# Layer norm's chain, the first gate block, the token shift and one mask placed elsewhere in a fused attention and feed-forward kernel

## The reference

```python
x = x + ffn(cond(x, cond_2048, ...))          # x: (128, 32, 128) float32
# cond: convolution, layer norm, a 32-step recurrence, gate, output product
# ffn, six layers, each:
def attn_layer(x, Wqkv, qs, ksc, Wo):         # 16 heads of 64, windows of 32 tokens
    q, k, v = split(x @ Wqkv)                 # 128 -> 3 * 1024
    q, k = l2norm(q) * qs, l2norm(k) * ksc    # then rotary, scaled by position
    out = softmax(mask(q @ k.T * 8)) @ v
    return out @ Wo
def ffn_layer(x, g, bln, W1, b1, W2, b2):
    xn = layer_norm(x) * g + bln
    a, gate = split(xn @ W1 + b1)             # 128 -> 2 * 341
    return a * gelu(gate) @ W2 + b2
for i in range(6):
    x = attn_layer(shift_tokens(x), ...) + x  # shift: half of the channels come from the token before
    x = ffn_layer(shift_tokens(x), ...) + x
```

## Time and profile before

| | us |
|---|---|
| three runs, median (lowest to highest) | 2849.02 (2846.26 to 2850.98) |
| the profiled execution | 2847.98 |
| its span | 2846.2 |
| in it, TensorE busy | 2691.9 (95%) |
| VectorE busy | 2600.1 (91%) |
| ScalarE busy | 2246.7 (79%) |
| GpSimd busy | 2116.7 (74%) |

### The profile page before, as it was taken

The page is one execution under the profiler, slowest core; times in us unless marked ns, Lnnn a source line. Parts: engine busy times, 40 slices in busy tenths (PEclk is TensorE's granted clock), DMA queues, the critical chain, the costliest instruction groups (busy, mean ns, idle before and its releaser), DMA issues.

```text
span 2846.2 us, 92826 instructions
## 1 busy us (share of the span) xinstructions
PE 2691.9 (95%) x36416; PEld 2060.1 (72%) x36417; DVE 2600.1 (91%) x3375; ACT 2246.7 (79%) x3776; POOL 2116.7 (74%) x1529
## 2 busy tenths in 40 slices
PE   8799978999999999999999999999999999999996
PEld 7577756777777777777777777777777777777774
DVE  7899968999999999999999999999999999999993
ACT  5799957878788787878888787888878787887873
POOL 6766658777778777778777787777787777877771
PEclk9899999999999999999999999999999999999998
DMA  1000013232223332223232232222322322322222
GB/s 57 24 2 2 1 35 76 67 76 69 67 69 75 73 73 66 69 71 75 66 79 69 66 75 71 72 67 70 76 67 68 79 62 68 72 67 58 64 66 79
DMA packets 103719, 178.41 MB, mean 63 GB/s; under 512 B 29350, under 2 KB 52708, under 8 KB 103396
## 3 DMA queue, kind: packets, MB, share of 16 engines
q1 hardware_dynamic: 102372, 174.60, 25.2%
q10 hardware_dynamic: 1152, 1.20, 0.1%
HBM read 22.62 MB, written 2.10 MB: 9 GB/s over the span
## 4 chain that ended last, share of the span: by engine, by line
PE 30%; POOL 16%; issue 15%; ACT 11%; DMA 7%; DVE 5%; SPq 1%; POOLq 0%; ACTq 0%; DVEq 0%
PE pa L843 9%; POOL spare L1446 8%; DMA kT<-spare 7%; PE px L872 5%; PE pg L982 3%; PE ps L903 3%; PE pg L960 3%; PE px L917 3%; PE pg L974 2%; POOL xs_lo L1432 2%; DVE ss L1269 2%; ACT spare L1095 2%; POOL pr L1484 2%; ACT spare L1041 1%; POOL spare L1455 1%
## 5 line engine op out<-in xcount | busy, mean ns | idle before, releaser
L1446 POOL TENSOR_TENSOR spare<-spare,qk_t 128x1024 f32<-128x1024 f32 x384 | 910.1, 2392 | 10.9 <-POOL xs_lo L1432 8.1
L843 PE MATMUL pa<-w_hi,xs_hi 128*128 128x512 f32 x1152 | 511.9, 444 | 25.3 <-issue 8.6
L1462 POOL TENSOR_TENSOR sm<-sm,inv 128x512 f32<-128x512 f32 x192 | 201.8, 1051 | 429.2 <-DVE sm L1307 361.4
L1285 DVE TENSOR_TENSOR qk_t<-pa,rot 128x1024 f32<-128x1024 f32 x384 | 464.6, 1210 | 1.6 <-ACT spare L1048 0.8
L1276 DVE TENSOR_TENSOR spare<-pa,rot 128x1024 f32<-128x1024 f32 x384 | 464.6, 1210 | 0.0
L1269 DVE TENSOR_REDUCE ss<-spare 128x16 f32<-128x1024 f32 x384 | 457.7, 1192 | 6.1 <-ACT spare L1041 5.2
L843 PE MATMUL pa<-w_hi,xs_lo 128*128 128x512 f32 x1152 | 459.2, 399 | 0.3 <-DMA pT<-prT 0.3
L843 PE MATMUL pa<-w_lo,xs_hi 128*128 128x512 f32 x1152 | 455.0, 395 | 0.0
L872 PE MATMUL px<-ident_sb,spare 128*128 128x128 f32 x3072 | 407.2, 276 | 18.8 <-POOL spare L1455 11.9
L1455 POOL TENSOR_TENSOR spare<-spare,inv 128x1024 f32<-128x1024 f32 x192 | 365.9, 1905 | 69.6 <-ACT inv L1080 65.3
L872 PEld LDWEIGHTS px<-ident_sb,spare 128*128 128x128 f32 x3072 | 340.4, 140 | 105.1 <-issue 44.6
(11 more groups left out here) (178 smaller groups left out, 5926.1 us busy)
## 6 DMA issues: line engine op xcount, KB each, us to landing
kT<-spare SPq DMA_DIRECT2D x384, 256.0 KB, 3.7
pT<-prT SPq DMA_DIRECT2D x768, 64.0 KB, 2.0
w_part<-in_Wqkv SPq DMA_DIRECT2D x40, 192.0 KB, 3.7
wo<-in_Wo SPq DMA_DIRECT2D x6, 512.0 KB, 5.5
c_h<-in_x SPq DMA_DIRECT2D x4, 512.0 KB, 9.5
spare<-in_x SPq DMA_DIRECT2D x8, 256.0 KB, 4.8
out<-spare SPq DMA_DIRECT2D x8, 256.0 KB, 2.5
wo<-in_W SPq DMA_DIRECT2D x6, 341.0 KB, 5.2
```

What stands on the lines that cost most here:

```text
L843: last = pe.matmul(pa[(u + c) % 2][:, half * 512:half * 512 + 512], x[:, j * P:(j + 1) * P], w[:, at], start=(k == 0), stop=(k == 2))
L1285: dve.tensor_tensor(halves(qk_t[:, c, :]), halves(pa[(3 * j + c) % 2][:])[:, :, ::-1, :], table.unsqueeze(1).to_broadcast([P, HEADS, 2, DH ...
L1446: pool.tensor_tensor(qk_r[:, c, :], qk_r[:, c, :], qk_t[:, c, :], ALU.add)\
```

## The change

Five things, all in `stack`:

1. The chain of layer norm. TensorE's `variance` goes from behind the key transposes of step 0 to between the two halves of `project_k` of that step. ScalarE's `log_variance` goes ahead of `square_k`, and `round_normed` ahead of `floor_norms` and `copy_v`. VectorE's `normalise` goes ahead of the key's `sum_squares`, and `rest_of_normed` ahead of `rest_of_outputs`.
2. `gate_block(i, 2, 0)` goes from behind `scores` and `transpose_q` of step 1 to ahead of `scores`, right behind `project_q`.
3. The shift is done in three parts (256, 128 and 128 tokens). ScalarE does the second at step 3 of the body before and the third at step 0, behind `inverse_deviation`; GpSimd likewise, behind `norm_keys`.
4. The mask of the scores of step 1 is written by a bf16 matmul of TensorE in front of them, and ScalarE no longer writes it at step 0.
5. The reciprocal of the denominators goes behind `rest_of_outputs` at steps 0, 1 and 2.

```diff
-        HALF_TOK = 2 * P
+        SHIFT_PART = ((0, 2 * P), (2 * P, P), (3 * P, P))
...
-                def project(i, j, c, full, l, before_last=None):
+                def project(i, j, c, full, l, before_last=None, between=None):
...
                     for half in range(2):
+                        if between and half == 1:
+                            between()
...
-                        if j % 2 == 0:
-                            pe.wait_ge(s["xs_ready"], 4 * i + j + 2)
+                        if j != 1:
+                            pe.wait_ge(s["xs_ready"], 6 * i + (2 if j == 0 else 2 * j))
...
-                        project(i, j, 1, "k_full", l)
+                        project(i, j, 1, "k_full", l, None, (lambda: variance(i, 2)) if j == 0 else None)
+                    elif j == 0:
+                        variance(i, 2)
...
-                def scores(i, j, back):
-                    n, j, live = tile(i, j, back)
-                    if live:
-                        if isinstance(n, int) and n == 0:
+                def scores(i, j_now, back):
+                    n, j, live = tile(i, j_now, back)
+                    if live:
+                        if j_now == 1:
+                            pe.wait_ge(s["sub_done"], n)
+                        if j_now == 1 or isinstance(n, int) and n == 0:
                             pe.matmul(ps[:], ident_b[:], mask_b[:], start=True, stop=False, skip_group_check=True)
-                        wait_for(pe, s["masked"], n)
+                        else:
+                            pe.wait_ge(s["masked"], {0: i * 3 - 1, 2: i * 3, 3: i * 3 + 1}[j_now])
...
                         project_q(i, j, l)
+                        if j == 1:
+                            gate_block(i, 2, 0)
                         if j == 2:
                             a_block(i, 2, 1)
                         scores(i, j, 2)
                         if j == 0:
                             subtract_mean(i, 2)
                         transpose_q(i, j, 1)
-                        if j == 1:
-                            gate_block(i, 2, 0)
...
                         transpose_k(i, j, 1)
-                        if j == 0:
-                            variance(i, 2)
...
# ScalarE
                         if j == 0:
-                            shift_hi(i, 0, 1)
-                        if j == 2:
-                            shift_hi(i, -1, 0)
+                            log_variance(i, 2)
+                        if j >= 2:
+                            shift_hi(i, -1, j - 2)
...
-                        if j == 0:
-                            log_variance(i, 2)
...
-                        write_mask(i, j, 1)
+                        if j > 0:
+                            write_mask(i, j, 1)
                         if j == 0:
                             inverse_deviation(i, 2)
+                            shift_hi(i, 0, 2)
                         exponentials(i, j, 2)
...
                         copy_oT(i, j, 3)
+                        if j == 0:
+                            round_normed(i, 2)
                         floor_norms(i, j, 0)
...
-                        if j == 0:
-                            round_normed(i, 2)
# VectorE
                         times_cos(i, j, l, 1, "sq_k", "tk_done", "cos_k")
+                        if j == 0:
+                            normalise(i, 2)
                         sum_squares(i, j, 0, 1, "sq_k", "sum_k")
                         if j == 3:
                             add_attention(i, 1)
-                        if j == 0:
-                            normalise(i, 2)
                         if j == 1:
                             gated(i, 2, 0)
                         denominators(i, j, 2)
+                        if j == 0:
+                            rest_of_normed(i, 2)
+                        if j == 3:
+                            reciprocals(i, j, 2)
                         rest_of_outputs(i, j, 3)
+                        if j < 3:
+                            reciprocals(i, j, 2)
                         if j == 1:
                             gated(i, 2, 1)
-                        if j == 0:
-                            rest_of_normed(i, 2)
# GpSimd
                         if j == 0:
-                            shift_lo(i, 0, 1)
+                            shift_lo(i, 0, 2)
+                        if j == 3:
+                            shift_lo(i, -1, 1)
```

More of the change, by code:

```diff
@@ L1133, in tables, with shift_hi @@
                         act.preload_act_table_set(name)
-                def shift_hi(i, back, half, first=False):
+                def shift_hi(i, back, part, first=False):
                     g, live = group(i, back)
@@ L1138, in shift_hi @@
                     if live:
-                        at = bass.ds((g % GROUPS) * GTOK + half * HALF_TOK, HALF_TOK)
-                        to = slice(half * HALF_TOK, (half + 1) * HALF_TOK)
+                        first_tok, toks = SHIFT_PART[part]
+                        at = bass.ds((g % GROUPS) * GTOK + first_tok, toks)
+                        to = slice(first_tok, first_tok + toks)
                         act.wait_ge(s["res_ready"], g + 1)
-                        wait_for(act, s["v_full"], g * GT - 2 * (1 - half))
+                        wait_for(act, s["v_full"], g * GT - (2 - part))
                         act.copy(xs_hi[0:64, to], res[0:64, at]).then_inc(s["xs_hi_ready"], 1)
@@ L1259, in _ @@
                         shift_hi(0, 0, 1, True)
+                        shift_hi(0, 0, 2, True)
                 group_steps(act, body, lambda l: None)
@@ L1314, in denominators, with reciprocals @@
                         dve.reduce_sum(den[:], keys(pr[:]), AX.X).then_inc(s["den_done"], 1)
+                def reciprocals(i, j, back):
+                    n, j, live = tile(i, j, back)
+                    if live:
                         dve.wait_ge(s["den_done"], n + 1)
@@ L1424, in _, with shift_lo @@
             def _(pool):
-                def shift_lo(i, back, half, first=False):
+                def shift_lo(i, back, part, first=False):
                     g, live = group(i, back)
@@ L1428, in shift_lo @@
                     if live:
-                        at = bass.ds((g % GROUPS) * GTOK + half * HALF_TOK, HALF_TOK)
-                        to = slice(half * HALF_TOK, (half + 1) * HALF_TOK)
-                        chunk = 2 * g + half
+                        first_tok, toks = SHIFT_PART[part]
+                        at = bass.ds((g % GROUPS) * GTOK + first_tok, toks)
+                        to = slice(first_tok, first_tok + toks)
+                        chunk = 3 * g + part
                         rest = lambda dst, src: pool.tensor_tensor(dst, src, hi, ALU.subtract)
@@ L1530, in _ @@
                 shift_lo(0, 0, 1, True)
+                shift_lo(0, 0, 2, True)
                 pool.wait_ge(first_loaded, 3 * 16)
```

## The result

The changed kernel takes 2891.52 us (median of 4 runs, 2891.18 to 2893.52), the kernel before 2850.00 on the same chip: ratio 1.0146, 95% interval 1.0129 to 1.0164.

A forecast was written before the change was run, and what follows sets the result against it. TensorE, 95% busy, bounds the kernel, with its step 1 gap waiting for the keys. 30 x 0.85 + 16 x 0.15 - 1.5 = +26.4 us on 2847.98, 2874.4, plus 1.04 to the median: 2875 us, range 2855 to 2893.

The forecast's parts named there:

- The deciding step: TensorE at step 1: gate block waits 1.45 us for VectorE's `fn_lo`, replacing 1.01 us for keys; `project_k` 0.7 us later.
- the lateness of that chain: VectorE's chain from step 0, held by `square_k` ending about 0.25 us later: 0 to 0.3 us, taken as 0.05.
- regular bodies: Groups 3 to 7 of each layer, 30 in all, with a 0.82 to 0.88 us gap at step 1; 0.85 us lost each.
- the lateness of `times_sin` for `project_v`: VectorE starts step 1 about 1.05 us late, so q's `times_sin` holds `project_v`: 0 to 0.3 us more, taken as 0.15.
- The other groups: The 16 other groups amid projections, with step 1 gaps of 0.75 to 2.1 us: 0.15 us lost each.
- The tail: Body 48, without projections: gate blocks earlier, last scores behind the first of them; -1.5 us, bounds -3 and +2.
- rival C: Late reciprocal delays GpSimd's normalising, key scaling and `transpose_k` of step 2: 0.4 us more per group, 2893 us; chance 0.14.
- TensorE has no slack from step 1 on: Outside the step 1 gap TensorE never visibly pauses, so time added or removed around step 1 enters the group's length.
- Rival A: `fn_lo` is there when TensorE asks, scores start when the keys land, `project_k` 0.5 us earlier: 2820 us; chance 0.14.
- what is late next: Keys for step 1's scores land at 1543.3 instead of 1542.9; late next if the gate block did not wait.
- Edit 3: Shift in three parts: extra fixed cost on ScalarE and GpSimd falls in idle places; 0, bounds -0.2 and +0.2 us a group.
- edit 5: Later reciprocals: VectorE saves 0.1 us three times a group, GpSimd's normalising 0.8 us later; worth 0, bounds -0.3 and +0.3.

The follow-up runs named there:

- c1: Changed kernel with `round_normed` ahead of `copy_oT` on ScalarE and `rest_of_normed` ahead of `denominators` on VectorE, so `fn_lo` comes earlier; 2871.8 us, ratio 1.0073.
- a3: Changed kernel with edit 5 alone undone, each reciprocal again right behind its denominators; 2902.2 us, ratio 1.0177.
- b2: Kernel before with edit 3 alone, the shift in three parts; 2847.9 us, ratio 0.9988.
- a5: Changed kernel with the first gate block behind the scores and `transpose_q` in body 48 alone; 2891.3 us, ratio 1.0122.
- d1: Kernel before with edits 3 and 5, the shift in three parts and the reciprocals behind `rest_of_outputs`; 2846.1 us, ratio 0.9980.
- a1: Changed kernel with edit 2 alone undone, the first gate block again behind scores and `transpose_q` of step 1; 2881.8 us, ratio 1.0110.
- a6: Changed kernel with the first gate block again behind scores and `transpose_q`, and `rest_of_normed` again behind `rest_of_outputs`; 2862.0 us, ratio 1.0038.
- a7: Changed kernel with gate block and `rest_of_normed` back, plus `variance` again behind the key transposes and `log_variance` behind the keys' copy; 2842.3 us, ratio 0.9952.
- b1: Kernel before with edit 2 alone, the first gate block ahead of the scores of step 1; 2985.6 us, ratio 1.0484.

## Why the prediction was right

**The deciding step held.** `fn_lo` is too late for the gate block: forecast 1.45 us of standing from 1541.98, measured 1.26 shown plus the 0.15 by which the 0.86 shown before was less than my 1.01, so 1.41. c1 shows that the wait costs, a3 that it grows with what delays `fn_lo`.

**Its sizes.** `project_k` of step 1: forecast 0.7 late, measured 0.80. The scores in front of it start 13.05 us after those of step 0 where I had 12.85, since `fn_lo` is 0.1 later and the mask takes 0.32 instead of 0.25; from the scores to `project_k` it is 1.88 instead of 2.00, since the transposes of q no longer wait 0.15 for `oT_lo`. `project_q` of step 1 starts 0.2 later, released by VectorE's rotary product of the keys. I had put the lateness of that chain at 0.05, and had looked for it in ScalarE's squares alone. The rows show GpSimd: its normalising (POOL) and VectorE's transpose of the probabilities at step 0, before and then changed:

```profile
1532.20 1.05 POOL L1484 TENSOR_TENSOR pr<-pr,rden 128x512 f32<-128x512 f32 x1
...
1533.42 0.70 DVE L1294 STREAM_TRANSPOSE prT<-pr 128x512 f32<-128x512 f32 x1
```

```profile
1553.45 1.05 POOL L1500 TENSOR_TENSOR pr<-pr,rden 128x512 f32<-128x512 f32 x1
...
1554.66 0.71 DVE L1301 STREAM_TRANSPOSE prT<-pr 128x512 f32<-128x512 f32 x1
```

From the start of the scores of step 0 the normalising ends at 1.60 and 1.81 us, the transpose starts at 1.77 and 1.97. In a3, with the reciprocals back, the normalising ends at 1.63 in the regular bodies: it is edit 5 that makes it 0.2 late. (With that gone, a3's VectorE waits for the squares instead, and `project_q` is still 0.17 late.) Then the lateness of `times_sin` for `project_v`: its row ends at 1570.37 + 1.21 = 1571.58 and `project_v` starts at 1571.64, 0.25 further lost where I took 0.15. A regular body lost 1.07 instead of 0.85: 6.6 us in all.

**The other groups** lost 0.54 instead of 0.15, 6.2 us. I had worked out one of them, the one whose scores start at 1592.98, and taken it for all 16. For that one the sum came out (`project_k` 15.08 us after the scores of step 0, against 14.89). On the average of the 16 `project_k` starts 0.44 later (15.31 against 14.87), by body from 0.6 earlier to 1.9 later, and neither kernel is alike over the 16: the gap for the keys before is 0.8 us in some and 2.1 in others, and in the changed kernel `project_k` starts between 14.9 and 16.1 us. Behind it `project_v` loses 0.22 more, as in the regular groups, and I had given that too little.

**The tail** came out at +4.1 instead of -1.5, 5.6 us, and the start at +0.8. With these the 19 us between forecast and measured spans are accounted for, but the tail's part is no finding: b2 has a body 48 of the same length as a5 without any move of the gate block.

**How close it was.** The forecast was +26 us and the medians give +41.5, at the very top of the range and next to rival C's 2893. That it lies inside is owed to wide bounds. What speaks for the forecast and not for C is not the time but c1 and a3, and the gate block's wait in the trace.

**What was wrong in the reasoning, though not in the forecast.** I said that TensorE has no slack from step 1 on and treated the wait for the keys as the one thing in its way. b2 and d1 show a second holder right behind it, `oT_lo` from VectorE: with the keys 0.4 us earlier the time moved by 0.1%. Rival A, "the scores start when the keys land ... 2820 us", left it out as well; no run has A's case, so what A would have kept of its 29 us is not shown. And I did not name what `rest_of_normed` pushes back on its own engine. In the changed kernel this is masked: `oT_lo` ends at 1564.49 + 1.21 = 1565.70, and behind the late scores the transposes of q start only at 1566.77. With the gate block back it shows.

Undone one after the other, in ratios to before: the gate block's place gives 0.36% (a1), `rest_of_normed` 0.72% (a6), the early variance 0.86% (a7), and what is left of the change is 0.48% faster than before. That is 10, 20 and 25 us lost and 14 gained, the 41.5 us of the whole. The parts hold in this order only: alone in the kernel before, the gate block costs 134 us. So the forecast named the wait that ends last in the changed kernel. Of the two further losses behind it, both larger once that wait is away, it named the later keys of the early variance as what is late next (landing 0.4 us later), and the delay of `oT_lo` not at all.

**Edit 3** at 0 and **edit 5** at 0 with bounds of 0.3: edit 3 held. Edit 5 is worth 0.3 us a group in the changed kernel, because the reciprocal would else stand ahead of `rest_of_normed`; that was in my own number for `fn_lo` (1542.6, not 1542.9) but not in the price of the edit. By the rule weighed there (the Trainium skill, VectorE: DVE Perf Modes, "The DRAIN you can't avoid") the split would free nothing on VectorE. In the changed kernel the denominators take 1563.83 - 1563.24 = 0.59 us from start to start where they took 0.71, so 0.1 us a time is freed. I had left out a sentence of that section: a next instruction that is not held starts earlier. With it the 0.1 us is no contradiction.

## What to carry to other kernels

An instruction put ahead to cover a wait has to be ready when that wait begins: work out the end of its own input chain, engine by engine, before moving it, since in an in-order stream it otherwise holds everything behind it. Putting a chain in front on an engine that has no idle time moves the loss to whatever was behind, so name the consumer of each instruction passed (here `px`, by way of `oT_lo`). A wait that shows in the profile may have a second one just behind it; shorten it alone before counting on it. And a sum worked out on one group holds for the groups that look like it: here the 16 others differed among themselves by more than the sum was worth.

## What the runs showed of the hardware that I had not expected

A wait of TensorE of 2.6 us amid full work (b1) brought the granted clock down in 17 of the 30 regular bodies and left it alone in 13, and where it came down the body was 1.2 us longer, about half of the wait's own length once more. A wait of 1.26 us did so in none of the 30 (changed kernel). And body 48, the first without projections, where TensorE works and pauses by turns, took between 43.1 and 48.6 us in single profiles, by the clock granted there (0.88 to 0.68) and not by the order of its instructions alone.
